# Router scores taken by VectorE from the normalised rows, in place of split matmuls with two columns on TensorE

## The reference, cut to what matters

```python
# in reference(), after layer 0
xn = _layernorm(x, axis=-1)                       # 2048 x 512
x = x + _L1_attn_ref(xn, ...) + _L1_ffn_ref(xn, ...)

def _L1_ffn_ref(hidden_states, w_router, ...):
    scores = jnp.einsum('btd,d->bt', hidden_states, w_router)   # one number a token
    _, idx = jax.lax.top_k(scores, k)                           # k = 256
    ...                                                         # attention and MLP over the chosen
    gate = jax.nn.sigmoid(sel_scores).reshape(S, 1)
```

## Time and profile before

| | us |
|---|---|
| median of 3 runs | 1689.16 (1688.1 to 1695.2) |
| profiled execution, its own time | 1688.49 |
| its span | 1686.7 |
| TensorE busy over the span | 1561.0 (93%) |
| VectorE, ScalarE, GpSimd busy | 1018.6, 713.4, 449.8 |
| mean granted TensorE clock | 0.965 of full speed |

### The profile page before, as it was taken

How to read it: one execution, slowest core, us unless ns; L and a number is a source line. 1 busy time by engine, 2 the same in 40 slices (tenths; PEclk the granted TensorE clock), 3 DMA queues, 4 the chain that set the end, 5 groups by cost and what they waited for, 6 DMA issues and landing times. The chain is left out here.

```text
span 1686.7 us, 23276 instructions
## 1 busy us (share of the span) xinstructions
PE 1561.0 (93%) x7008; PEld 1069.7 (63%) x7008; DVE 1018.6 (60%) x2743; ACT 713.4 (42%) x1202; POOL 449.8 (27%) x662
## 2 busy tenths in 40 slices
PE   5999999999999998799878999999999988999898
PEld 4887888887666776577644545555554536646484
DVE  5453666666555545799867776666668755575121
ACT  5533665655553333233224445655555531116010
POOL 0001777776101323422311112221221232130000
PEclk9999999999999999899959999999999998999899
DMA  4002212121002323467692404404413206514201
GB/s 169 1 1 82 104 69 103 68 103 51 13 25 69 119 75 126 114 172 201 190 281 115 107 7 110 96 26 108 111 26 90 61 14 202 194 50 200 99 1 12
DMA packets 96825, 158.74 MB, mean 94 GB/s; under 512 B 7956, under 2 KB 59220, under 8 KB 89176
## 3 DMA queue, kind: packets, MB, share of 16 engines
q1 hardware_dynamic: 92216, 147.28, 28.4%
q0 software_dynamic: 2208, 6.10, 1.4%
q10 hardware_dynamic: 2304, 4.20, 0.6%
HBM read 114.67 MB, written 42.87 MB: 93 GB/s over the span
## 5 line engine op out<-in xcount | busy, mean ns | idle before, releaser
L1958 ACT ACTIVATE l_pt<-banks 128x1024 f32<-128x1024 f32 (+3 forms) x288 | 218.5, 811 | 161.6 <-PE banks L1839 159.6
L2027 DVE CUSTOM_DVE_ANT_0 stage<-banks,l_edges 128x384 f32<-128x384 f32 (+3 forms) x384 | 201.6, 541 | 101.6 <-issue 100.6
L1876 PE MATMUL banks<-l_pt,l_v 128*64 128x512 f32 (+3 forms) x1152 | 231.4, 524 | 2.5 <-POOL l_pt L1933 2.4
L699 POOL TENSOR_TENSOR ex_hl<-ex_h,ex_hh 128x512 fp32r<-128x512 f32 x128 | 165.7, 1301 | 81.0 <-ACT ex_hh L667 80.8
L1932 POOL TENSOR_TENSOR l_turn<-l_before 128x2 f32<-128x2 f32 x192 | 40.0, 208 | 423.3 <-ACT l_pt L1958 412.9
L2030 DVE TENSOR_REDUCE l_mx<-banks 128x1 f32<-128x384 f32 (+1 forms) x208 | 113.1, 544 | 51.0 <-PE banks L1817 50.2
L733 DVE SCALAR_TENSOR_TENSOR ex_rw<-banks,ex_wb 128x512 f32<-128x512 f32 x128 | 88.3, 691 | 79.0 <-PE banks L75 78.9
L1876 PEld LDWEIGHTS banks<-l_pt,l_v 128*64 128x64 f32 x1152 | 70.6, 140 | 96.4 <-issue 72.7
L667 ACT ACTIVATE ex_hh<-ex_h 128x512 fp32r<-128x512 f32 x128 | 80.9, 632 | 103.5 <-DVE ex_h L741 102.0
L1817 PE MATMUL banks<-k,q 96*128 96x384 f32 (+3 forms) x296 | 93.9, 409 | 18.1 <-PEq L2664 7.7
L73 PE MATMUL banks<-ex_xlh,ex_wh 128*128 128x512 f32 x256 | 101.6, 397 | 2.0 <-DVE ex_rw L733 2.0
(11 more groups left out here) (400 smaller groups left out, 3416.7 us busy)
## 6 DMA issues: line engine op xcount, KB each, us to landing
ex_wb<-gates_by_expert SPq DMA_DIRECT2D x16, 1024.0 KB, 4.7
layer_v<-qkv_vs SPq DMA_DIRECT2D x16, 512.0 KB, 3.2
layer_qk<-qkv_yh SPq DMA_DIRECT2D x32, 256.0 KB, 3.7
layer_qk<-qkv_yl SPq DMA_DIRECT2D x32, 256.0 KB, 4.0
l_v<-layer_v SPq DMA_DIRECT2D x8, 1024.0 KB, 16.4
ex_ws<-ew_in SPq DMA_DIRECT2D x16, 384.0 KB, 4.9
l_q<-layer_qk SPq DMA_DIRECT2D x12, 512.0 KB, 8.0
l_k<-layer_qk SPq DMA_DIRECT2D x12, 512.0 KB, 13.3
```

Of the source, the lines that this page charges most:

```text
L699: pool.tensor_tensor(hl[:, k % RING, :], h[:, k % RING, :], raw(hh[:, k % RING, :]), ALU.subtract).then_inc(hl_done, 1)
L1876: last = pe.matmul(bank[h * 2 * HD:(h + 1) * 2 * HD, (qa - b * BT) * P:(qz + 1 - b * BT) * P], v[par][:, kt, h, :], pt[:, step_part(b, j), ...
L1958: act.activation(pt[:, step_part(b, j), :, 0:width], G.banks[:, 2 * slot:2 * slot + 2, 0:width], ACT.Exp, scale=scale).then_inc(p_done, 1)
L2027: dve.tensor_tensor_reduce(cutoff[:, n % 4, 0:width], G.ps[5 + n % MB][:, 0:width], masked, 1.0, NEG, ALU.add, ALU.max, mx[:, h, m, c:c + ...
```

## The change

Each score becomes the sum of products of a token's 512 normalised values with the router's weights, taken on VectorE from `xn` as it stands (tokens on partitions), one `scalar_tensor_tensor` with an accumulator a tile, right behind `low(t-1)` and ahead of `scales(t)`. The weights are now loaded as one row broadcast to 128 partitions. The 48 matmuls, the row copies, the 16 small transposes, the column copies and four stores of rows are gone. ScalarE's `normal(t)` waits also for the score of tile t-3, since that reads the buffer of `xn`. At the head of `stage_qkv` TensorE turns the 128x16 scores into 16x128, ScalarE copies them to SBUF ahead of its first weight split, and SyncE stores them once, after tile 4. Lines of the code after are some 60 lower in this stage.

```diff
-        wr, wrh, wrl = M.sb("wr", [P, NC]), M.sb("wrh", [P, NC, 2], F32R), M.sb("wrl", [P, NC, 2], F32R)
+        xn, wr, weighed = M.sb("xn", [P, RING, D]), M.sb("wr", [P, D]), M.sb("weighed", [P, D], BF16)
...
-            sp.dma_start(wr[:, :], I["w_router"]).then_inc(wr_in, 16)
+            sp.dma_start(wr[:, :], I["w_router"].partition_broadcast(P)).then_inc(wr_in, 16)
...
-                    if n == 6:
-                        pe.wait_ge(row_sb, 1)
-                        pe.wait_ge(pair_sb, 1)
...
-                    if b >= 1 and k == 1:
-                        scores(b - 1)
-                    if b >= 1 and k == 2:
-                        pairs(b - 1)
             queries(0)
             transposes(NT - 1)
             queries(1)
-            scores(NB - 1)
-            pairs(NB - 1)
...
                 wait(act, res_ready, t - RING + 1)
+                wait(act, sc_done, t - RING + 1)
...
-                if b >= 1 and k == 1:
-                    score_row(b - 1)
...
+            def score(t):
+
+                if t == 0:
+                    dve.wait_ge(wr_in, 16)
+                dve.wait_ge(xn_ready, t + 1)
+                dve.scalar_tensor_tensor(weighed[:, :], xn[:, t % RING, :], 1.0, wr[:, :], ALU.mult, ALU.mult,
+                                         accum_out=G.score[:, t:t + 1]).then_inc(sc_done, 1)
...
-                if b >= 1 and k == 3:
-                    score_columns(b - 1)
                 total(t)
                 variance(t)
                 if t >= 1:
                     low(t - 1)
+                    score(t - 1)
                 scales(t)
...
             low(NT - 1)
-            score_columns(NB - 1)
-            dve.wait_ge(pair_sb, NB)
+            score(NT - 1)
+            dve.wait_ge(sc_done, NT)
... stage_qkv
+                if t == BT:
+                    sp.wait_ge(score_sb, 1)
+                    sp.dma_start(S.score.rearrange("(t p) -> t p", p=P), scores).then_inc(score_out, 16)
...
+            pe.transpose(G.ps[7][0:NT, 0:P], G.score[:, :], G.ident[:, :]).then_inc(score_mm, 1)
             keys(0)
...
+            act.wait_ge(score_mm, 1)
+            act.activation(scores, G.ps[7][0:NT, 0:P], ACT.Copy).then_inc(score_sb, 1)
             weights.high(act)
```

More of the change, by code:

```diff
@@ L956, in stage_output0 @@
         G.sem("b_" + n) for n in ("var", "sd", "rstd", "xn", "xt", "hi", "lo", "res", "link"))
-    wr_in, wrh_done, wr_done, sc_mm, row_sb, pair_mm, pair_sb, r_stored = (G.sem("b_" + n) for n in (
-        "wr_in", "wrh", "wr", "sc_mm", "row_sb", "pair_mm", "pair_sb", "r_stored"))
+    wr_in, sc_done, r_stored = (G.sem("b_" + n) for n in ("wr_in", "sc", "r_stored"))
     RING = 3
     xn_stored = [G.sem(f"b_xn_stored{n}") for n in range(RING)]
-    row_stored = [G.sem(f"b_row_stored{n}") for n in range(2)]
     with ExitStack() as stack:
@@ L1057, in _ @@
                 sp.wait_ge(xn_stored[n], 16 * len(range(n, NT, RING)))
-            for n in range(2):
-                sp.wait_ge(row_stored[n], 16 * NB // 2)
         @block.gpsimd
@@ L1120, in transposes @@
                 last.then_inc(xt_ready, 1)
[L1122 to L1133, removed]
-                mm3(pe, score_banks(b)[0][0:2, :], [((wrh[:, c, :], wrl[:, c, :]), (G.xTh[:, c, cols], G.xTl[:, c, cols]))
-                                                    for c in range(NC)]).then_inc(sc_mm, 1)
-            def pairs(b):
-                pe.wait_ge(row_sb, b + 1)
-                for k in range(BT):
-                    last = pe.transpose(score_banks(b)[1][:, 2 * k:2 * k + 2], row[:, b % 2, k * P:(k + 1) * P],
-                                        G.ident[0:2, 0:2])
-                last.then_inc(pair_mm, 1)
             def queries(t):
@@ L1213, in high @@
                                ACT.Copy).then_inc(hi_ready, 1)
-            def score_row(b):
-                act.wait_ge(sc_mm, b + 1)
-                if b >= 2:
-                    act.wait_ge(row_stored[b % 2], 16 * (b // 2))
-                act.activation(row[:, b % 2, :], score_banks(b)[0][0:2, :], ACT.Copy).then_inc(row_sb, 1)
             rectified(0)
@@ L1310, in _ @@
             lows(2)
-            dve.wait_ge(wr_in, 16)
-            for n in range(2):
-                last = dve.tensor_copy(wrh[:, :, n:n + 1], wr[:, :].unsqueeze(2))
-            last.then_inc(wrh_done, 1)
-            dve.wait_ge(wrh_done, 1)
-            for n in range(2):
-                last = dve.tensor_tensor(wrl[:, :, n:n + 1], wr[:, :].unsqueeze(2), raw(wrh[:, :, n:n + 1]), ALU.subtract)
-            last.then_inc(wr_done, 1)
+            dve.memset(G.score[:, :], 0.0)
             for t in range(NT):
                 b, k = t // BT, t % BT
-                if b >= 1 and k == 3:
-                    score_columns(b - 1)
                 total(t)
@@ L1347, in stage_qkv @@
         G.sem("qkv_" + n) for n in names)
-    tab_in, first_in = G.sem("qkv_tab_in"), G.sem("qkv_first_in")
+    tab_in, first_in, score_mm, score_sb, score_out = (
+        G.sem("qkv_" + n) for n in ("tab_in", "first_in", "score_mm", "score_sb", "score_out"))
     qk_out, v_out = ([G.sem(f"qkv_{n}{k}") for k in range(2)] for n in ("qk_out", "v_out"))
@@ L1362, in stage_qkv @@
         vs = M.sb("vs", [P, 2, H0, 2 * HD])
+        scores = G.kvb[0:NT, 0, :]
         gam = t2[:, 0, 0:4 * HD].rearrange("p (k m d) -> p k m d", k=2, m=2)
@@ L1411, in transposes @@
                     wait(pe, hl_done, 2 * (t - 1) + k + 1)
+                    if t == 0 and k == 1:
+                        pe.wait_ge(score_sb, 1)
                     for g in range(NC):
```

19 lines of the change are left out of this document (2 added, 17 removed).

## The result

| | before | after |
|---|---|---|
| median of 20 runs, us | 1691.72 (1683.8 to 1696.34) | 1697.4 (1690.63 to 1706.25) |
| ratio to before | | 1.0038, 95% interval 1.0025 to 1.0051 |
| profiled execution, span in us | 1688.49, 1686.7 | 1695.78, 1693.8 |
| TensorE, VectorE busy, us | 1561.0, 1018.6 | 1554.3, 1031.9 |
| mean granted clock | 0.965 | 0.963 |

The change costs 6.4 us by the ratio (4.2 to 8.6, by the interval; the two medians lie 5.7 apart); the forecast was 2.8. The sign and the case (a loss within what one measurement can tell) came as forecast, the size is more than twice. The time forecast was 1692.0, from 1684.5 to 1699.5, and 1697.4 lies inside. Of the 5.4 us between them 2.6 are not the change's: the median of three runs that the forecast started from, 1689.16, is 1691.72 over twenty.

A forecast was written before the change was run, and what follows sets the result against it. The stage was taken as two chains of nearly equal length, TensorE's and VectorE's. 4.4 (blocks) - 3.7 (stage's end) + 1.5 + 0.6 (clock) = 2.8 us slower, 1691.3 as profiled, 1692.0 as median; range 1684.5 to 1699.5.

The forecast's parts named there:

- TensorE bound throughout: Rival for the whole stage: all that TensorE loses arrives as gain, 15.9 us, giving 1673.3; chance 0.05.
- The signs that the prediction named: Profile: `xn` waits 10 us or more, scores about 0.75, half clock behind tile 6, stage's end about 4 us nearer.
- The price of a score: On VectorE between `low` and the reciprocal, each score holds the next instruction 0.66 us; lower bound 0.60.
- The upper bound of 1.35: Highest price of a score in us, if the 0.35 us of 128 elements grow fourfold for 512.
- The port: Block 0, tiles 1 and 2: GpSimd's addition holds the score as it held the shift; 1.0 us later each.
- The rival in which the port does not hold a score and the clock stays: Block 0 costs 0.3 in place of 2.0, the 0.6 and the clock's 2.1 go: 1687.6 us; chance 0.18.
- Block by block: TensorE goes on 2.0 us later in block 0, 0.8 earlier in 1, 1.4 later in 2, 1.2 in 3.
- The clock: Half speed behind the 3.3 us wait in tile 6 costs 1.5 us; behind the last transposes 0.6.
- Port waits in block 3: Blocks 2 and 3 together: 0.6 us estimated, between nothing and 1.29 in each of two tiles.
- The head: Start of `stage_qkv`: added transposition and copy hide behind VectorE's 4.07 us wait for GpSimd's tables; costs nothing.
- The stage's end: Behind the last transposes: column copy and row stores go, the residual's store comes last; gain 3.7 us, from 3.0 to 4.4.
- Scores are dear: Rival: twelve scores on the path at 1.35 in place of 0.66, 8.3 us more, or more port waits: 1700.3; chance 0.15.

The follow-up runs named there:

- without scores: The changed kernel with the sixteen score instructions left out and zeros written for the scores; ratio to before 0.9996 (0.9982 to 1.0010).
- scores behind the shift: The changed kernel with the score of tile t-1 moved behind the shift of tile t, same work; ratio to before 0.9994 (0.9978 to 1.0009).
- without the additions: The changed kernel without GpSimd's additions of layer 0's output bias; ratio 1.0010 (0.9993 to 1.0027).
- before with sums: The kernel before, its TensorE scores kept, plus sixteen unread sums of products on VectorE at the change's place; ratio 1.0074 (1.0047 to 1.0101).
- after with the later head: The changed kernel with the scores' transposition and copy in `stage_qkv` moved behind the first value product and squares; ratio to before 1.0061 (1.0038 to 1.0084).
- after with matmuls: The changed kernel with twelve unread matmuls a block where the scores of blocks 0 to 2 had stood; ratio to before 1.0035 (1.0016 to 1.0053).
- before without additions: The kernel before without GpSimd's additions of layer 0's output bias; ratio 0.9974 (0.9953 to 0.9995).
- 36 unread matmuls: The changed kernel with score behind the shift, later transposition and copy in `stage_qkv`, and twelve unread matmuls a block; ratio to before 0.9973 (0.9955 to 0.9990).

## Why the prediction was right, and where its sizes were off

**The mechanism held.** TensorE's matmuls were not what set the stage, and VectorE's chain was: without scores the blocks gain 1.2 us, with scores behind the shift they gain 2.5, and only scores ahead of the reciprocal lose. The rival "TensorE bound throughout" (1673.3), which had 12.2 arriving in the blocks, is refuted by the kernel without scores: 661.29 against 662.48. The signs that the prediction named came, but for the length of a lone score: 0.68, not 0.75.

**The price of a score** was 0.66, is 0.61: near the lower bound, a product without an accumulator. The reading of the accumulator (0.08) hides. (The upper bound of 1.35 should have been 1.32, four times 0.35 less the overlap of 0.08; nothing hangs on it.)

**The port.** The prediction held that GpSimd's addition holds a score, from the shift in the earlier trace rows; the score of 1.77 beside an addition of 1.28 shows it, and its absence without the additions confirms it. By the Trainium skill ("SBUF — State Buffer", section "Who interferes with whom") the instruction that starts first keeps the shared port until it ends; the traces agree, in tile 2 with GpSimd first and in tile 1 with the score first. There the addition, begun 0.09 to 0.35 into the score, ends 1.20 or 1.21 behind the start of the accumulator's reading in four executions (after, before with sums, after with the later head, after with matmuls). The rival in which the port does not hold a score and the clock stays (1687.6) is out on both counts: scores are held, and the clock falls even without GpSimd's additions (1.12 for the transposes of tile 6).

**Block by block.**

| "later", us | forecast | measured |
|---|---|---|
| block 0, at the transposes of tile 2 | 2.0 | 1.87 |
| block 0, clock behind tile 2 | 0 | 1.64 |
| block 1, `total` 4 to `total` 8, clock in it | -0.8 + 1.5 | 0.66 |
| block 2, `total` 8 to start of block 3 | 1.4 + 0.3 | 1.62 |
| start of block 3, `total` 12, clock | 0 | 1.48 |
| block 3, `total` 12 to last transposes | 1.2 + 0.3 | 2.85 |
| last transposes to GpSimd's first load | -3.7 (+ 0.6 clock) | -4.61 |
| from there to the step behind the tables | 0 | 1.85 |
| sum | 2.8 | 7.36 |

"Measured" is the difference between two executions; a row of it can be off by more than a microsecond, as the 1.64 in block 0 was 0 in the like kernel with the later head. Blocks 0 to 2 were worked out right where VectorE's chain decides. Three terms were mis-sized.

*The clock*, 1.5 + 0.6 in the sum. Its price for one drop was right (block 1 comes out as forecast), the number of drops was not: the prediction took only waits of three us or more as ones that bring half clock. In block 0 it came behind 1.56 and 2.18, one tile apart; at the start of block 3 behind 3.12 and 1.84, where the prediction had the matmuls behind tile 10 hidden by VectorE's chain and did not ask what the clock would be when block 3 began. Together 3.1 us. The drop in block 3, behind a wait of 2.19 in tile 13, costs nothing that shows, and the 0.6 behind the last transposes did not come: the clock is full there until 680 us.

*Port waits in block 3.* The prediction allowed 0.3 there and placed them on the score. They came on the shift behind it, 1.02 and 1.07 us in tiles 13 and 14, where before's shifts took 0.16 and 0.50: 1.4 more.

*The head.* "These do not hang on ScalarE: nothing". The tables don't, but GpSimd's loads land later, and the multiplications on them took 5.42 in place of 4.96: 1.85. Part of it is not the change's, as the spread over kernels shows. The stage's end gave 0.9 more than forecast in return.

**The rival on the other side.** "Scores are dear" forecast 1700.3 by a price of 1.35 or by more port waits. The time, 1697.4, lies nearer to it than to 1692.0, but that is the base's shift: as a loss against before, 6.4 lies between 2.8 and 11.1, a little nearer to 2.8. Its price is refuted (0.61). Of its mechanisms the clock's share is what came true, and with it the port's in block 3.

## What to carry to other kernels

Ask of an instruction that is added to an in-order engine what stands right behind it, not what it costs: the same sixteen cost 12.6 us of the stage or nothing, one place apart. Work taken from an engine that is busy 93% of the time gains little where another engine's chain is as long, and there its going can cost, since the idle time that it leaves can bring the clock of what remains down (about 1.5 us a time here, in three of four places, and not only behind the longest wait). Where VectorE and GpSimd shared a port here, one of the two became longer in either order. And a gain that a stage's rows show has to be looked for in the median too: 4 to 5 us of it were gone here 780 us later.

## What the runs showed of the hardware that was not expected

- Waits of 1.56 and 2.18 us one tile apart brought TensorE to 1.2 GHz, and so did 1.58 and 2.13 (before with sums on VectorE); 1.57 and 2.12 (after with the later head) and 1.59 and 2.04 (after with matmuls) did not. In tile 6 one of 2.01 did not in the earlier trace rows, and one of 2.00 did in before without additions; one of 2.52 did with the score behind the shift, and one of 2.56 did not without scores. At such lengths the wait alone does not settle it.
- 36 unread matmuls kept the clock full from 528 us to the last transposes (1.00, against 0.97 without them) and shortened the way there from `total` of tile 4 by 2.1 to 2.2 us, by one execution with them and two without; the kernel with them is 0.27% (0.10 to 0.45) faster than before.
- With the score first, GpSimd's addition took 1.60 in place of 1.29, and VectorE's next two-input instruction (one element) waited until it ended.
